# Involution: first residuals on ScalarE's queue, first token tiles loaded by planes

## What is computed

```
x = x + L0_conv(ln_c(x), ...)
...
red = einsum('bchw,oc->bohw', x, w_reduce) + b_reduce
ker = einsum('bohw,ko->bkhw', red, w_span) + b_span
ker = ker.reshape(B, G, K * K, H, W)
xp = pad(x, 6 on each side)
patches = [xp[:, :, i*DIL : i*DIL+H, j*DIL : j*DIL+W] for i, j < K]
out = einsum('bgckhw,bgkhw->bgchw', patches, ker)
```

## Time and profile before

| | |
|---|---|
| median of 3 runs | 2967.88 us (2960.94 to 2973.62) |
| the profiled execution | 2962.64 us, span 2960.9 us |
| TensorE busy | 2353.1 us, 79% of the span |
| VectorE, ScalarE, GpSimd busy | 50%, 44%, 10% |
| `apply_b` L459 | 4096 matmuls, 154.7 us busy |
| `make_b` L438 | 2048 matmuls, 149.6 us busy |
| VectorE L501 | 256 instructions, 484 ns each |
| `inv_x` loads | 88 on SP, 88 on GpSimd, 112 KB each |
| `inv_xo` loads | 32 on SP, 256 KB each |

### The profile page before, as it was taken

The page is one execution under the profiler, slowest core; times in us unless marked ns, Lnnn a source line. Parts: engine busy times, 40 slices in busy tenths (PEclk is TensorE's granted clock), DMA queues, the critical chain, the costliest instruction groups (busy, mean ns, idle before and its releaser), DMA issues. The chain is left out here.

```text
span 2960.9 us, 78991 instructions
## 1 busy us (share of the span) xinstructions
PE 2353.1 (79%) x34528; PEld 1793.6 (61%) x34528; DVE 1494.5 (50%) x3491; ACT 1310.6 (44%) x2623; POOL 301.9 (10%) x586
## 2 busy tenths in 40 slices
PE   0465889934534999999999999999877785789898
PEld 0334888822213888888888888888733652344444
DVE  6341343423341666666666555665511253377777
ACT  0463243425302666666656656665511264333332
POOL 0112111200020000000000000000012001022221
PEclk9765798967787999999999999999999697799999
DMA  6437455632353111111111111100088630000000
GB/s 196 126 113 117 86 102 99 116 128 114 133 126 103 43 43 43 43 43 43 43 43 43 43 43 40 42 21 18 23 267 277 223 93 13 5 23 23 24 21 28
DMA packets 183365, 235.04 MB, mean 79 GB/s; under 512 B 35820, under 2 KB 142825, under 8 KB 179513
## 3 DMA queue, kind: packets, MB, share of 16 engines
q1 hardware_dynamic: 150117, 120.85, 15.4%
q0 software_dynamic: 29024, 90.96, 11.5%
q10 hardware_dynamic: 3888, 18.25, 1.6%
HBM read 141.68 MB, written 88.31 MB: 78 GB/s over the span
## 5 line engine op out<-in xcount | busy, mean ns | idle before, releaser
L947 DVE COPY spc_g<-spc_pz 128x512 f32<-128x512 f32 x1024 | 629.0, 682 | 311.9 <-PE spc_pz L843 311.8
L917 ACT ACTIVATE spc_g<-spc_pz 128x512 f32<-128x512 f32 x1024 | 549.4, 612 | 284.4 <-PE spc_pz L843 284.0
L843 PE MATMUL spc_pz<-spc_v,spc_as 108*128 108x128 bf16 x8192 | 554.2, 219 | 16.6 <-issue 3.3
L843 PEld LDWEIGHTS spc_pz<-spc_v,spc_as 108*128 108x128 bf16 x8192 | 473.9, 97 | 105.3 <-ACT spc_g L917 32.7
L864 PE MATMUL spc_pz<-spc_g,spc_u 128*20 128x128 f32 x16384 | 469.1, 274 | 21.5 <-DVE spc_g L947 17.3
L864 PEld LDWEIGHTS spc_pz<-spc_g,spc_u 128*20 128x20 f32 x16384 | 451.1, 135 | 48.3 <-ACT spc_g L917 30.1
L1454 PE MATMUL moe_ex<-moe_ew,moe_d 128*128 128x512 f32 x512 | 249.9, 611 | 33.0 <-DVE moe_yt L1611 32.6
L828 PE MATMUL spc_pu<-spc_f,spc_s 128*128 128x256 f32 x768 | 207.5, 395 | 71.9 <-DMA spc_s<-s_sf 71.9
L1611 DVE SCALAR_TENSOR_TENSOR moe_yt<-moe_ex,moe_gb,moe_yt 128x128 f32<-128x128 f32 x768 | 209.7, 343 | 103.3 <-ACT moe_yt L1513 102.0
L501 DVE SCALAR_TENSOR_TENSOR inv_xo<-inv_pa,inv_mask,inv_xo 128x256 f32<-128x256 f32 x256 | 123.6, 484 | 228.8 <-PE inv_pa L459 167.4
L479 ACT ACTIVATE inv_b<-inv_pb 112x1024 f32<-112x1024 f32 x128 | 125.4, 1021 | 228.2 <-PE inv_pb L438 228.2
(11 more groups left out here) (201 smaller groups left out, 2231.0 us busy)
## 6 DMA issues: line engine op xcount, KB each, us to landing
s_yd<-spc_yo SPq DMA_DIRECT2D x128, 160.0 KB
s_sf<-fwd_so ACTq DMA_DIRECT2D x16, 1024.0 KB, 5.3
spc_s<-s_sf POOLq DMA_DIRECT2D x32, 512.0 KB, 6.4
ivs_y<-s_yd POOLq DMA_DIRECT2D x32, 512.0 KB, 5.2
s_td<-ivs_to SPq DMA_DIRECT2D x32, 512.0 KB, 4.7
ln_t<-s_td SPq DMA_DIRECT2D x32, 512.0 KB, 3.8
inv_x<-s_xn SPq DMA_DIRECT2D x88, 112.0 KB
inv_x<-s_xn POOLq DMA_DIRECT2D x88, 112.0 KB, 8.1
```

Source lines behind the costliest of these rows:

```text
L843: m = pe.matmul(pz[:, (p + 2) % 3, e // 4, 2 * FT * (e % 4):2 * FT * (e % 4) + 2 * FT], AS[:, x, 8 * p + e, :], V[:, k, x, :, FT * t:FT * ...
L917: act.activation(g_out(p, 0), g_in(p, 0), ACT.Copy).then_inc(ga, 1)
L947: v.tensor_copy(g_out(p, 1), g_in(p, 1)).then_inc(gd, 1)
```

## The change

Three things change, all in the first loads of `involution`.

- The residuals of phases 0 and 1 are issued by ScalarE, as the first thing it does in the block. SP issues the others as before, with their waits.
- The first token tiles are loaded by `tile_in`: one transfer for each tw, band and plane instead of one for each tw, band and row. It fills all 112 partitions with 2 KB each, 224 KB. There are 16 on SP and 16 on GpSimd.
- TensorE's wait for a token tile counts from 64 instead of 128, since four transfers instead of eight raise the semaphore.

```diff
+        def tile_in(eng, band, tw):
+            for plane in range(4):
+                src = S["XN"][16 * band:16 * band + 8, plane // 2, plane % 2, 8 * tw:8 * tw + ROW].rearrange(
+                    "r w b c -> r w (b c)")
+                eng.dma_start(X[:, tw, band, plane].rearrange("w b c -> w (b c)"), src).then_inc(x_in[band][tw], 16)
+
+        def residual(eng, n):
+            for band in range(2):
+                eng.dma_start(xo[64 * band:64 * band + 64, n % 2], strip(I["x"], band, n // 2, n % 2)).then_inc(xo_in[n % 2], 16)
...
@@ SP
-            def residual(n):
-                if n >= 2:
-                    sp.wait_ge(xo_out[n % 2], 32 * (n // 2))
-                for band in range(2):
-                    sp.dma_start(xo[64 * band:64 * band + 64, n % 2], strip(I["x"], band, n // 2, n % 2)).then_inc(xo_in[n % 2], 16)
-
             for tw in range(4):
-                for row in range(8):
-                    rows_in(sp, 0, 0, row, tw)
-            for n in range(3):
-                residual(n)
+                tile_in(sp, 0, tw)
+            sp.wait_ge(xo_out[0], 32)
+            residual(sp, 2)
...
                 for n in (2 * s + 1, 2 * s + 2):
                     if n < NPH:
-                        residual(n)
+                        sp.wait_ge(xo_out[n % 2], 32 * (n // 2))
+                        residual(sp, n)
@@ GpSimd
             pool.memset(Wz[:], 0.0).then_inc(cleared, 1)
             for tw in range(4):
-                for row in range(8):
-                    rows_in(pool, 1, 0, row, tw)
+                tile_in(pool, 1, tw)
@@ TensorE
                     for band in range(2):
-                        pe.wait_ge(x_in[band][tw], 128 + 32 * s)
+                        pe.wait_ge(x_in[band][tw], 64 + 32 * s)
@@ ScalarE
+            residual(act, 0)
+            residual(act, 1)
             for n in range(NPH):
```

## The result

| | before | changed |
|---|---|---|
| median of 8 runs each | 2969.05 us (2952.79 to 2989.11) | 2940.74 us (2926.60 to 2950.27) |
| ratio, with its 95% interval | | 0.9898 (0.9867 to 0.9930) |
| the profiled execution | 2962.64 us, span 2960.9 us | 2950.27 us, span 2948.5 us |

The change saves 28.3 us between the medians, 1.0%; the forecast was 2944 us and faster. The profiled executions are only 12.4 us apart.

A forecast was written before the change was run, and what follows sets the result against it. Late residual and token loads at the involution's start were taken to hold TensorE for 27.9 us; phase 1 gains 21.9 plus 2 for the clock, other terms 0, so 2967.9 - 24 = 2944 us, range 2930 to 2966.

The forecast's parts named there:

- the 24 us that I put on phase 1: Start of the involution's phase 1: 21.9 us earlier, plus 2 for a possible faster clock in phase 0.
- The 18.25 us wait for the residual goes.: Involution phase 0: TensorE's 18.25 us wait vanishes; ScalarE's four residual issues take 2.5 us, covered before its first copies.
- 0 to 3.1 us, I take 0: Stage start: residuals' 1.05 MB compete with w_span and mask loads, shifting everything 0 to 3.1 us; taken as 0.
- 8 engines at 169 GB/s: First token loads: each transfer on 8 engines at 21.1 GB/s; with alternating halves the last tile lands at 279.5.
- The 9.8 GB/s of an engine in the old form: Old token loads: a busy engine's speed, put down to all engines writing into 14 partitions.
- Tile 0 by 255.: First token tile: 1.90 MB on the fuller half of the engines takes 11.2 us, landing at 255.
- TensorE.: Phase 0: starts near 261.6, low-clock pairs of 7.37 us, then 1.16 us wait; phase 1 at 292.2, 21.9 us earlier.
- Nothing of a later stage is loaded ahead, so what phase 1 gains the end gains.: After phase 1 starts: each phase waits for the one before, so its gain carries to the end.
- 12.5 us either way: Later involution phases: one low-clock episode of TensorE more or less moves the time 12.5 us; taken as 0.
- the slower one: Token loads: half the engines at today's speed; phase 1 15 us later, 2983, or 39 slower, 3007; chance 0.08.
- The unchanged total of 149 GB/s: First loads: something beyond the partitions holds them; phase 1 at 308.6, 5.5 us earlier, 2962; chance 0.12.
- Rival 3: First loads: GpSimd's on SP's eight engines at 21.1 GB/s; phase 1 at 298.8, 15.3 us earlier, 2953; chance 0.10.

The follow-up runs named there:

- the second profile: The changed kernel profiled and timed once more, unchanged: ratio 0.9921 (0.9888 to 0.9953); the kernel before was likewise repeated: ratio 0.9984 (0.9958 to 1.0009).

## Why the prediction came out right

The time was right, 2940.7 for 2944, and the sign and the main mechanism too. That the figure came so close is luck: of the 24 us that I put on phase 1 some 15 came, and some 9 came at the exit, which I had put at nothing.

- *The 18.25 us wait for the residual goes.* Right: VectorE's wait is gone. ScalarE's four issues took 2.94 us, from 243.01, where I had 2.5, and were covered.
- *The small loads, "0 to 3.1 us, I take 0".* Wrong end: the matrices of phase 0 start 2.8 us later, 2.4 of them within the stage. Putting the residuals behind the mask gave these back.
- *The tiles, "8 engines at 169 GB/s".* The number of engines for SP's stream was right. That GpSimd's transfers alternate between the halves fits the shares (1.05 while both queues are full, 0.53 behind), though no view names the engines; but both halves together move only 200 GB/s and not twice 169. The 9.8 GB/s of an engine in the old form, which I gave to the 14 partitions, is no constant of that form either: with the residuals moved alone it was 177 / 16 = 11.1. The loads are over near 286, not at 279.5.
- *"Tile 0 by 255."* The step that failed most. I divided the bytes of the fuller half by its speed, as if the streams were served in the order of need. SP's stream got 1.02 of 4.75 MB in the first 23 us, and tile 0 of band 0 came near 269 (265.5 in the second profile). With everything on one queue it came by 262.6. The first application started 7.6 us later than the 261.6 that I had put, 2.8 of them from the matrices, and tile 1 cost 1.2 us more.
- *TensorE.* Cold pairs of 7.30 us and the 1.1 us wait nearly as put; the clock did not rise in phase 0 of the first profile, so the 2 us that I added for it were not there (in the second it was 0.71 from 268 to 276 us). Phase 1 came 13.2 and, in the second profile of each, 17.4 us earlier, mean 15.3, for 24.
- *"Nothing of a later stage is loaded ahead, so what phase 1 gains the end gains."* True of the loads, but I costed the exit of the block at nothing. It gives 8.8 us, and it is in all seven profiles with GpSimd's 16 plane transfers and the later rows. 15.3 + 8.8 = 24.1 us; the two sets of runs gave ratios of 0.9898 and 0.9921, that is 30 and 23 us, with intervals of some 10 us either way.
- *"12.5 us either way" for the clock.* Right in kind and too small: the middle stretch of the unchanged queues spans 35 us (267 to 302). Whether its mean is longer with the planes cannot be told: the three profiles with the rows on both queues have 278 to 282, the seven with the planes on GpSimd and unchanged later rows 274 to 302. The medians, which average over it, leave room for at most some us.

Of the rivals, the slower one (8 engines at 9.8 GB/s each) is refuted: 8.5 engines move 200 GB/s. The unchanged total of 149 GB/s is refuted too: 203 GB/s from 245 to 285, where the kernel before moved 145. Rival 3, GpSimd on the same eight engines at 21.1, did not happen, but when I forced it by putting all on SP, phase 1 came at 298.7; I had worked out 298.8, with 21.1 GB/s an engine in place of 23.5, so that agreement is partly luck.

## What to carry to other kernels

A transfer that is waited for late may be late because of what stands ahead of it. Here either moving it or speeding up what was ahead did, and the two did not add. A wait that goes can also take a faster clock with it, so cost the work behind it at both levels. When loads of several queues compete, compute the arrival of the first tile from what its own queue gets, not from the total, and put small loads that open a stage ahead of big ones (2.4 us at the start here, though phase 1 came no earlier). Cost the end of a block as well: look which engine arrives last at the barrier and with which instruction, since a change of that engine's transfers moved it by 8.8 us here, where the work that was aimed at gave some 15.

## What the runs showed of the hardware

- GpSimd's drain at the end of a block took 1.04, 2.67, 3.17, 7.09, 8.56 or 9.86 us, always the same for the same stream of GpSimd's transfers, with all its stores landed. Its cause is open.
- SP's loads whose source counts 8 outermost and whose target counts 112 keep 8.5 of 16 engines busy, and move 200 GB/s with them; GpSimd's in the same form keep sixteen busy and move 202 to 217.
- The same 2 KB pieces into 14 partitions at a time moved 149 GB/s at a share of 0.95 and 177 GB/s at 1.00 with the residuals moved alone; into 112 partitions from a source of 112 pieces they moved 275 GB/s at 1.05. The ports of SBUF (SBUF — State Buffer, "Door 1: The DMA port swizzle" in the Trainium skill) would fit the first; no run here separates them from the source's layout.
- A pause of TensorE of 0.5 to 3.6 us in its own instruction stream can be followed by 24 to 36 us at 1.2 GHz with TensorE busy but for the 1.1 us between two phases, in a phase that takes 17 us at 2.4 GHz. Two in three of the pauses stand at the same seven places of its list, whatever the version.
- The same 15 phases took 267 us at a mean granted clock of 0.92 and 302 at 0.81, with the same instructions in the same order.
